# Pass 2 of a fused spectral and Sobel layer: the first axis of the step three ahead goes between the stencil's two directions, and the opening alternates the axes

## The reference

```python
# layer 0: discrete Hartley transform, 20 x 20 modes kept, channels mixed by weights, transform back
x = x + _L0_conv_ref(_gn(x), L0_conv_weights1)
# layer 1: depthwise Sobel filter, gradient magnitude
x = x + _L1_conv_ref(_gn(x))
...
gx = conv(x, wx); gy = conv(x, wy)
return jnp.sqrt(gx * gx + gy * gy + EPS)
```

## Time and profile before

| | us |
|---|---|
| median of 3 runs | 2219.04 (2218.7 to 2219.3) |
| the profiled execution, its own time | 2217.58 |
| span of the profiled execution | 2215.8 |
| TensorE busy | 2150.8 |
| ScalarE busy | 1962.3 |
| VectorE busy | 1773.7 |
| GpSimd busy | 1602.3 |

### The profile page before, as it was taken

One profiled execution on the slowest core, in us unless ns is written; L12 is line 12 of the kernel. 1 busy time (PEld: TensorE's weight loads), 2 busy tenths in 40 slices (PEclk: granted clock), 3 DMA queues, 4 the chain that ended last, 5 costly groups with the idle time before them and its releaser, 6 DMA issues.

```text
span 2215.8 us, 55005 instructions
## 1 busy us (share of the span) xinstructions
PE 2150.8 (97%) x20520; PEld 1574.0 (71%) x20520; DVE 1773.7 (80%) x2703; ACT 1962.3 (89%) x3691; POOL 1602.3 (72%) x929
## 2 busy tenths in 40 slices
PE   5999999999998699999999999999999999999998
PEld 4888888888887566666666666666666666666665
DVE  4889899898975668878878877877877887887777
ACT  5999999999975488999999899899899999989998
POOL 4777777777752287777777777777777777777776
PEclk9999999999999799999999999999999999999999
DMA  7777777777764346666666666566666666666664
GB/s 210 220 214 216 214 213 218 213 217 212 215 161 90 77 142 182 181 196 187 184 194 190 181 187 198 177 192 190 189 190 190 187 179 193 195 181 190 192 193 138
DMA packets 808227, 414.77 MB, mean 187 GB/s; under 512 B 20784, under 2 KB 807216, under 8 KB 807344
## 3 DMA queue, kind: packets, MB, share of 16 engines
q1 hardware_dynamic: 807984, 411.43, 64.7%
HBM read 277.13 MB, written 134.22 MB: 186 GB/s over the span
## 4 chain that ended last, share of the span: by engine, by line
PE 64%; DVE 0%; issue 0%; ACT 0%; POOLq 0%; POOL 0%; DVEq 0%; ACTq 0%
PE g_ps L1213 45%; PE y_ps L1205 10%; PE v_ps L1193 7%; PE v_ps L1179 1%; DVE xbuf L1352 0%; POOLq L1040 0%; POOL p_lo L1147 0%; DVE g_ps L1358 0%; ACT g_ps L1280 0%; ACT p_hi L1261 0%; ACT g_ps L1286 0%; ACT v_sb L1267 0%; DVE xbuf L1364 0%; DVEq L1040 0%; ACTq L1040 0%
## 5 line engine op out<-in xcount | busy, mean ns | idle before, releaser
L1213 PE MATMUL g_ps<-p_hi,stencil 128*128 128x512 f32 x2048 | 851.0, 416 | 2.5 <-POOL p_lo L1147 2.5
L1147 POOL TENSOR_TENSOR p_lo<-pairs,p_hi 128x1032 fp32r<-128x1032 f32 x256 | 617.2, 2411 | 302.8 <-ACT p_hi L1261 302.8
L1213 PE MATMUL g_ps<-p_lo,stencil 128*128 128x512 f32 x2048 | 810.7, 396 | 0.0
L1213 PEld LDWEIGHTS g_ps<-p_hi,stencil 128*128 128x128 f32 x2048 | 386.3, 189 | 279.1 <-POOL p_lo L1147 142.0
L1358 DVE TENSOR_TENSOR g_ps<-gx,g_ps 128x512 f32<-128x512 f32 x512 | 350.4, 695 | 247.4 <-ACT g_ps L1280 247.0
L1142 POOL TENSOR_TENSOR pairs<-xbuf 128x1032 f32<-128x1032 f32 x256 | 488.5, 1908 | 26.3 <-DVE xbuf L1352 6.5
L1364 DVE SCALAR_TENSOR_TENSOR xbuf<-xbuf,rows,g_ps 128x256 f32<-128x256 f32 x1024 | 439.5, 477 | 36.2 <-ACT g_ps L1286 30.4
L343 POOL TENSOR_TENSOR m_lo<-xbuf,m_hi 128x512 fp32r<-128x512 f32 x256 | 306.3, 1197 | 191.9 <-ACT m_hi L457 191.8
L1213 PEld LDWEIGHTS g_ps<-p_lo,stencil 128*128 128x128 f32 x2048 | 385.9, 188 | 78.0
L1286 ACT ACTIVATE g_ps<-g_ps,rows 128x256 f32<-128x256 f32 x1024 | 409.2, 449 | 21.5 <-DVE g_ps L1358 4.4
L1280 ACT ACTIVATE g_ps<-g_ps 128x512 f32<-128x512 f32 x512 | 305.5, 602 | 84.6 <-PE g_ps L1213 82.8
(11 more groups left out here) (139 smaller groups left out, 2287.9 us busy)
## 6 DMA issues: line engine op xcount, KB each, us to landing
xbuf<-x SPq DMA_DIRECT2D x256, 512.0 KB, 5.2
xbuf<-x SPq DMA_DIRECT2D x512, 256.0 KB, 3.2
out<-xbuf SPq DMA_DIRECT2D x512, 256.0 KB, 2.9
wmix<-weights SPq DMA_DIRECT2D x8, 800.0 KB, 12.1
second_sb<-second SPq DMA_DIRECT2D x1, 1230.0 KB, 8.3
mats_sb<-mats SPq DMA_DIRECT2D x1, 832.0 KB, 6.8
first_sb<-first SPq DMA_DIRECT2D x1, 32.0 KB, 6.9
```

What stands on the lines that cost most here:

```text
L1147: nc.gpsimd.tensor_tensor(p_lo[:, r % 2, :, 0:W + 1], pairs[:, r % 2, :, 0:W + 1], p_hi[:, r % 2, :, 0:W + 1].bitcast(FP32), ALU.subtract) ...
L1213: mm = nc.tensor.matmul(g_ps[h][:, axis], stencil[:, m, :], p[:, r % 2, 4 * h:4 * h + 4, o:o + W], start=n == 0, stop=n == len(todo) - 1)
```

## The change

Four things move; no arithmetic is added or taken away.

1. In every step of pass 2 but the first, `first_axis(r+3)` leaves its place behind `second_axis(r+4)` and goes between the stencil's directions, behind the transposes where there are any. (In the first step it stood there already.)
2. At the opening of pass 2 TensorE does the second and the first axis of steps 0, 1 and 2 in turn, then the second of step 3; before, the second axis ran one step ahead. GpSimd's `neighbours` of step 2 goes behind its `low` of step 1.
3. In pass 1 the `stats` of tiles 0 to 13 are no longer made together, at the turn of tile 15, but one at each turn of a tile.
4. At the end of the stage between, the copies of the four wide banks stand among the last copies of coefficients, not behind them.

```diff
@@ pass1, second_axis
                 if k == 0:
                     pe.wait_ge(first_out, (i + 1) * HALVES + T_BANKS)
                     pe.wait_ge(modes_out, i + 1)
-                    for tile in range(TILES - 2) if i == TILES - 2 else range(i - 1, i) if i > TILES - 2 else ():
-                        stats(tile)
+                    if i:
+                        stats(i - 1)
@@ mix, ScalarE (VectorE likewise, with g == 4 or g == 6 and n = g - 3)
-            for n in range(0, 2 * TILES // WIDE, 2):
-                act.wait_ge(widened, n + 1)
-                a, h = divmod(n, TILES // WIDE)
-                nc.scalar.activation(out[:, a, h * per:(h + 1) * per], wide_ps[n], ACT.Copy)
+                if g == 5 or g == 7:
+                    n = g - 5
+                    act.wait_ge(widened, n + 1)
+                    a, h = divmod(n, TILES // WIDE)
+                    nc.scalar.activation(out[:, a, h * per:(h + 1) * per], wide_ps[n], ACT.Copy)
@@ pass2, GpSimd
                 if not beyond(i, r + 1):
                     low(i, r + 1)
+                if before(i, r, 1):
+                    neighbours(i, r + 2)
                 if not beyond(i, r + 3):
                     pool.wait_ge(lo_ready, at(i, r) + 2)
                     neighbours(i, r + 3)
...
             pool.wait_ge(lo_ready, 1)
-            neighbours(0, 2)
             over_steps(step)
@@ pass2, TensorE
             pe.wait_ge(coef_out, TGRP)
-            second_axis(0, 0)
-            second_axis(0, 1)
+            for r in range(3):
+                second_axis(0, r)
+                first_axis(0, r)
+            second_axis(0, 3)
             pe.wait_ge(setup, 1)
-            first_axis(0, 0)
-            second_axis(0, 2)
-            first_axis(0, 1)
-            second_axis(0, 3)
-            first_axis(0, 2)
 
             def step(i, r):
                 if not beyond(i, r + 4):
                     second_axis(i, r + 4, group(i, r - 1) if r else None)
-                if not beyond(i, r + 3) and not before(i, r, 1):
-                    first_axis(i, r + 3)
                 pe.wait_ge(lo_ready, at(i, r) + 1)
                 across(i, r, 0)
                 across(i, r, 1)
                 if group(i, r) is not None:
                     transposes(i, r, group(i, r))
-                if before(i, r, 1):
+                if not beyond(i, r + 3):
                     first_axis(i, r + 3)
                 down(i, r, 0)
                 down(i, r, 1)
```

More of the change, by code:

```diff
@@ L1029, in _ @@
                               tile0_ps[g % len(tile0_ps)][:, 0:n, :]).then_inc(tile0_out, 1)
[L1030 to L1033, removed]
+                if g == 4 or g == 6:
+                    n = g - 3
+                    dve.wait_ge(widened, n + 1)
+                    a, h = divmod(n, TILES // WIDE)
+                    V.tensor_copy(out[:, a, h * per:(h + 1) * per], wide_ps[n])
 def pass2(nc, sb, ps, sem, mat, x_p, out_p, mats, xpad, modes, groups, corner, mscale, x_in, coef, coef_t, coef_main,
```

## The result

The changed kernel takes 2353.97 us (2353.53 to 2354.95, 4 runs), the kernel before 2218.87; the ratio is 1.061, with a 95% interval of 1.0598 to 1.0622. The forecast was 2355, in a range of 2318 to 2385. The profiled execution has a span of 2351.9 us; the one before had 2215.8.

The account below looks back on a forecast made before the run. TensorE, busy for 97% of the span, was taken to bound the kernel. Plain steps 45, coefficient steps 25, transpose steps 67, pass 1 -1 and opening +1 sum to 137 us on 2217.6, given as 2355, range 2318 to 2385.

Parts of the forecast that it names:

- A second trip in 252 steps: Pass 2, TensorE: array use goes from full to halves and back twice per step, not once; +0.37 us each.
- plain steps: Pass 2, 120 steps without transposes or coefficient copies: across finds low done by 0.17 us; 5.84 us each, 45 us more.
- Steps with coefficient copies: Pass 2, 55 steps: low ends later than across wants it; 5.92 us a step, +0.45 each, 25 us.
- Steps with transposes: Pass 2, 77 steps: two covered waits, for copy_v and for VectorE's copy_coef, become visible; 67 us more.
- The ring: Steps with transposes: cycle from transposes through VectorE's copy_coef and add, roots and copy_v to the next transposes; 6.79 us, not 5.91.
- the ring's second half: Steps with transposes, the second wait: VectorE's order centre, copy_coef, add delays the second axis and add, which starts at 3.83.
- Pass 1: Turns of tiles: 9.3 us given back, 14 single stats cost 0.6 us each, 8.4; sum -1 us, bounds -9 and +2.
- Opening: Start of pass 2: first axis some 0.8 us earlier, but rounds stand in line; +1 us, bounds -2 and +3.
- the stage between: Each engine makes the same copies in another order; 0, at most 1 us either way.
- The trips alone: Rival, pass 2: waits absorbed, 252 x 0.37 = 93 us remain, 2312; chance of below 2335: 0.17.
- The spread of lateness to plain steps: Rival, pass 2: low comes 0.4 us later, so all steps lengthen; 2412 at worst; chance of over 2385: 0.1.
- The free second trip: Rival, pass 2: weights load ahead whatever array part is used, so the trip vanishes; 2210; chance 0.04.

Follow-up runs that it names:

- Experiment 7: Kernel before, first axis untouched; in 154 steps the second axis is cut in two, its first two products between the halves of the previous down: 2281.91 us, ratio 1.0282.
- experiment 6: Changed kernel with the first axis one place earlier, between the two halves of across: 2324.06 us, ratio 1.0473.
- experiment 4: Changed kernel with the transposes behind the first axis instead of ahead of it: 2320.19 us, ratio 1.046.
- experiment 5: Changed kernel with VectorE's copy_coef ahead of centre, its adding of the first axis, in steps with transposes: 2350.79 us, ratio 1.0593.
- Experiment 2: Changed kernel with the first axis of steps 1 and on back behind the second axis; opening, stats and copy order stay changed: 2215.05 us, ratio 0.9986.
- experiment 8: Kernel before with part 3 alone, stats once at each turn of a tile ahead of the second axis: 2212.94 us, ratio 0.9976.
- experiments 1: Kernel before with part 1 alone, the first axis between the stencil's directions in every step of pass 2: 2357.54 us, ratio 1.0631.

## Why the prediction was right, point by point

- **A second trip in 252 steps: shown.** Experiment 7 makes the trip without the first axis, experiment 6 puts the first axis elsewhere: 0.41 us each time in plain steps. Beside transposes it is 0.34 to 0.45, by the neighbours. The size was a little short: I had 0.37, and 5.84 us for a step that takes 5.88. The 117 plain steps of the table cost 49 us, and with the last steps 50, where 45 stood in the sum. The rule of the Trainium skill ("TensorEngine Tiling (Array Packing)", Key Properties: a change of the tiling mode drains the engine) agrees with the trace in that a change costs time, 0.41 us both ways. Whether a drain or an uncovered weight load makes it up, no run tells apart. What I had estimated from the figures of the Trainium skill's "TensorE: Matmul & The Clock Gate" (Step-by-step: what each phase is for; LDWEIGHTS), 0.32 us per step, is under the 0.41 measured.
- **Steps with coefficient copies: the size shown, the cause read in the trace.** 27.9 us, forecast 25. They take 333.8 / 56 = 5.96 us on average, forecast 5.92. In 42 of the 56 `across` starts just 0.05 us behind the end of `low`, and in most of these later in the step than the 0.64 us of a plain one. Added up from the starts this is 4.5 us; the other 23 are the trip (56 x 0.41). In experiment 7, which makes a trip in 55 of these steps but leaves `across` late, `low` has 0.3 us or more to spare. No run took the copies away.
- **Steps with transposes: shown, and a little oversized.** The ring was forecast at 6.79 us and is 6.69; its stations lie within 0.1 us of where they were worked out. I had added 0.11 us for the exposed load of the transposes' weights to the start of their row, but the row starts with the load. That is 7 x 10 x 0.1 = 7 us, about the difference between 67 and 61.2. Of the 61.2, 35 are trips in this order (27 in the order of experiment 4, 31 in that of experiment 6) and 26 are time in which TensorE stands. Most of the standing is seen in front of the second axis, for VectorE's copy. Yet experiment 5 takes that copy out and saves 4.3 us only; the wait for `v_sb` alone brings the step to 6.62. In the prediction the ring's second half sounded as heavy as the first; it isn't.
- **Pass 1: the sign right, the size short.** Forecast -1. Of the 3.8 us in the sum under the table, 1.5 come from the first tile, which the change doesn't touch, and the stage between takes 0.7 back; the turns themselves give 3.0. A turn with one `stats` takes 5.57 us, 0.45 more, where I had taken 0.6.
- **Opening: forecast +1, measured +0.7 to +3.9; the stage between: no effect seen.** Up to step 1 the five traces with the old opening take 18.6 to 18.7 us at a granted clock of 0.63 to 0.64. The new one takes 19.4 us at 0.65 in the changed kernel's trace, 20.9 to 21.1 at 0.59 in four others, and 22.6 at 0.55 in experiment 5. So the +0.7 is the lucky end of it. What goes with the lower clock was in no term of the sum. Experiment 2 (parts 2 to 4) is 2.1 us over experiment 8 (part 3), and in the traces the opening is 2.3 us longer. From the last `stats` to the first second axis the traces take 96.6 to 98.8 us with the old order of the copies and 96.5 to 98.0 with the new.
- **The rivals.** The trips alone would have been experiment 4's 2320: out by 34 us. The spread of lateness to plain steps didn't come: `low` is mostly 0.2 us ahead of `across` there, forecast 0.17. The free second trip is out by experiment 7.

Against the forecast of 137 us more, the profiled executions show 136 and the medians 135. The terms missed by +5, +3, -6 and -3 us, which largely cancelled. This is luck, and the 1 us between forecast and result says less than the three classes of steps do. (2219.04 and 137 are 2356; the 2355 was rounded the other way.)

## What to carry to other kernels

Count how often the program changes the way it uses the array, not only how many matmuls it issues: a group of matmuls on half the rows that is taken out of its neighbourhood costs a price on the way in and out, and no other engine can hide it on a TensorE that is always busy. Here it was 0.41 us for a group of 0.42 us and for one of 0.95, and 0.34 to 0.45 with transposes at a seam. In a profile such a price hides in the busy time; it is found in the distance from start to start at the seams, and in one group's duration behind different neighbours. Before a long instruction is moved past a shorter one that waits for something, look at what the long one covered: here 1 us of first axis hid a wait of 0.3 us, and of the 61 us that these steps lost, 26 are this wait and the ring that it closes.

## What the runs showed of the hardware that I had not expected

TensorE's granted clock falls in a stretch of one-column matmuls, although the engine shows no idle time there. Busy times, granted clock and DMA by windows, in the kernel before, where the 14 `stats` stand together from 615.31 to 623.3 us (columns: window, length, PE, PEld, DVE, ACT, POOL, granted clock, DMA share, GB/s):

```profile
617.00:619.00 2.00, 2.00 (x21) 2.00 (x20) 1.12 (x1) 0.52 (x1) 1.22 (x1) 1.00 0.73 200
619.00:623.00 4.00, 4.00 (x25) 4.00 (x24) 0.00 (x0) 0.00 (x0) 0.00 (x0) 0.59 0.67 179
623.00:625.00 2.00, 2.00 (x27) 1.87 (x28) 0.00 (x0) 0.00 (x0) 0.00 (x0) 0.50 0.00 0
```

And in the changed kernel, at the same place:

```profile
619.00:623.00 4.00, 4.00 (x62) 3.31 (x56) 3.74 (x5) 3.56 (x9) 2.48 (x3) 1.00 0.91 252
```

The engine is busy in all of these. Yet in the window from 619 us the granted clock falls to 0.5 of 2.4 GHz, the lower level (0.59 is a mean with the rest of full speed in it), while the engine does nothing but these matmuls, and it stays there into the products of 512 columns behind them. The traces of experiments 1 and 7, which have the same 14 `stats` together, show the same fall at this place. The eight traces with other code there show the full clock from 30 to 665 us. The other engines stand still in this stretch too, so that the matmuls' single column is the cause is likely and not shown.

What the lower clock costs can be read from starts. The first 40 of the 56 rows start 0.112 us apart, the later ones 0.213. The second axis and the first four matmuls of `mirror` behind them, with an ordinary turn first and the long one below:

```profile
536.34 0.92 PE L383 MATMUL r_ps<-second_sb,tmodes 128*64 128x40 f32 x24
537.19 0.50 PE L423 MATMUL z_ps<-m_hi,flips 128*128 128x512 f32 x1
...
538.25 0.40 PE L423 MATMUL z_ps<-m_hi,flips 128*128 128x512 f32 x1
...
623.26 1.54 PE L383 MATMUL r_ps<-second_sb,tmodes 128*64 128x40 f32 x24
624.74 0.80 PE L423 MATMUL z_ps<-m_hi,flips 128*128 128x512 f32 x1
...
626.60 0.40 PE L423 MATMUL z_ps<-m_hi,flips 128*128 128x512 f32 x1
```

At 0.112 us each the 56 rows would take 6.3 us, not 7.95 (615.31 to 623.26), and what stands behind them 1.91 us, not 3.34. So of the 9.3 us in the turn of 14.44 some 3.1 are the clock and some 6.2 the matmuls. Spread over the turns, the matmuls are paid all the same (14 x 0.45 = 6.3), and the 3 us that part 3 gains in these traces are about what the clock had cost.
